# Attention and mixture-of-experts layer: the last output projection ahead of the fifth group's routing, its residual and statistics ahead of the early search, the early ranks behind the last transposes

## The reference

```
x = x + cross_attention(layernorm(x), context, mask)     # 16 heads of 16, projected by Wo, plus bo
n = layernorm(x)                                         # 1792 rows of 256
gate_probs = softmax(n @ router_w)                       # 8 experts
topk_w, topk_idx = top_k(gate_probs, 2); topk_w /= sum   # two experts for each row
x = x + sum over the two of  weight * (silu(n @ w1[e]) @ w2[e])      # 256 -> 512 -> 256
```

## Time and profile before

| | |
|---|---|
| time, median of 3 runs | 452.66 us (452.36 to 453.35) |
| the profiled execution's own time | 451.87 us |
| its span, first to last instruction | 449.9 us |
| TensorE busy, weight loads busy | 411.5 us (91%), 382.5 us (85%) |
| VectorE, ScalarE, GpSimd busy | 336.4 us (75%), 279.8 us (62%), 223.9 us (50%) |
| share of TensorE in the chain that ended last | 79% |
| share of VectorE, of DMA in it | 9%, 5% |
| mean clock granted to TensorE | 0.959 of full |

### The profile page before, as it was taken

How to read it: one execution, slowest core, us unless ns; L and a number is a source line. 1 busy time by engine, 2 the same in 40 slices (tenths; PEclk the granted TensorE clock), 3 DMA queues, 4 the chain that set the end, 5 groups by cost and what they waited for, 6 DMA issues and landing times.

```text
span 449.9 us, 10827 instructions
## 1 busy us (share of the span) xinstructions
PE 411.5 (91%) x4219; PEld 382.5 (85%) x4219; DVE 336.4 (75%) x700; ACT 279.8 (62%) x381; POOL 223.9 (50%) x257
## 2 busy tenths in 40 slices
PE   7878999999999999999999996899999999999910
PEld 6747898999989999999998985789999999999910
DVE  7866778778877888787788778856886667776536
ACT  4767476665566665766555554648778777778600
POOL 6757443312444223433202764675787878876420
PEclk9999999999999999999999997589999999999975
DMA  7995676768866778766450259822222322332169
GB/s 213 237 199 155 135 158 131 150 150 162 197 159 156 153 140 189 157 132 128 96 120 3 75 205 365 272 68 73 85 80 85 95 83 94 83 82 73 47 231 306
DMA packets 44675, 64.32 MB, mean 143 GB/s; under 512 B 6801, under 2 KB 33570, under 8 KB 44626
## 3 DMA queue, kind: packets, MB, share of 16 engines
q1 hardware_dynamic: 38322, 50.40, 45.6%
q0 software_dynamic: 4096, 11.13, 8.2%
q10 hardware_dynamic: 2208, 2.12, 1.4%
HBM read 30.13 MB, written 9.28 MB: 88 GB/s over the span
## 4 chain that ended last, share of the span: by engine, by line
PE 79%; DVE 9%; DMA 5%; ACT 3%; issue 2%; POOL 1%; ACTq 0%; SPq 0%; DVEq 0%
PE ps L1546 41%; PE ps L1609 12%; PE ps L1626 9%; PE ps L1640 9%; PE ps L1915 2%; DVE x L1536 2%; PE ps L1653 2%; DMA q_stack<-attn_t_lo 1%; DMA y_back<-y_rows 1%; DVE neg_max L1105 1%; DMA keep<-keep_scratch 1%; PE ps L1709 1%; DMA keep_scratch<-keep_all 1%; PE ps L1665 1%; PE ps L1719 1%
## 5 line engine op out<-in xcount | busy, mean ns | idle before, releaser
L1105 DVE TENSOR_REDUCE neg_max<-ps 112x1 f32<-112x376 f32 x256 | 133.6, 545 | 41.4 <-PE ps L1609 36.5
L834 ACT ACTIVATE probs<-ps 125x1344 f32<-125x1344 f32 x64 | 82.8, 1294 | 43.4 <-PE ps L1626 38.2
L1609 PE MATMUL ps<-k_stack,q_stack 98*112 98x376 f32 x256 | 86.2, 369 | 3.7 <-DVE neg_max L1105 2.2
L604 POOL TENSOR_TENSOR k_lo<-k_f,k_hi 128x752 fp32r<-128x752 f32 x16 | 28.9, 1806 | 112.3 <-ACT k_hi L808 111.8
L765 POOL DMA_INDIRECT rows<-xn_rows,token_of_row x42 | 55.8, 1328 | 17.5 <-issue 12.5
L773 POOL DMA_INDIRECT y_rows<-y_out,slot_of_row x42 | 45.6, 1087 | 25.3 <-ACT y_out L1027 14.4
L1609 PEld LDWEIGHTS ps<-k_stack,q_stack 98*112 98x112 f32 x256 | 44.1, 174 | 16.3 <-DVE neg_max L1105 10.9
L1626 PE MATMUL ps<-q_stack,k_stack 100*125 100x224 f32 x384 | 52.6, 273 | 0.0
L1626 PEld LDWEIGHTS ps<-q_stack,k_stack 100*125 100x125 f32 x384 | 50.4, 188 | 0.7 <-ACT probs L834 0.5
L1546 PE MATMUL ps<-w_hi,h_hi 128*128 128x256 f32 x168 | 48.8, 290 | 0.4 <-DVE h_lo L1452 0.4
L1546 PE MATMUL ps<-flat_t_hi,w_hi 128*128 128x256 f32 x168 | 47.5, 283 | 1.3 <-DVE flat_t_lo L1430 1.3
(11 more groups left out here) (213 smaller groups left out, 1017.6 us busy)
## 6 DMA issues: line engine op xcount, KB each, us to landing
k_stack<-k_hi SPq DMA_DIRECT2D x32, 376.0 KB, 5.0
w_all<-w SPq DMA_DIRECT2D x2, 4096.0 KB, 18.8
k_stack<-k_lo SPq DMA_DIRECT2D x16, 376.0 KB, 5.5
ctx_raw<-ctx_t SPq DMA_DIRECT2D x32, 187.5 KB, 3.9
q_stack<-attn_t_hi SPq DMA_DIRECT2D x64, 56.0 KB
y_back<-y_rows SPq DMA_DIRECT2D x14, 256.0 KB, 5.1
x_rows_sb<-x_rows SPq DMA_DIRECT2D x4, 448.0 KB, 4.6
x<-x_tiles SPq DMA_DIRECT2D x7, 256.0 KB, 2.9
```

The costliest lines, as they stand in the source:

```text
L604: pool.tensor_tensor(kl[:, :, :], kf[:, :, :], kh[:, :, :].bitcast(F32), ALU.subtract)\
L834: act.activation(pf[j % 2][:, :, :], ps[0:CT, BK_ST:BK_ST + KT, 0:4 * S], ACT.Exp).then_inc(pf_ready, 1)
L1105: dve.tensor_reduce(neg_max[:, head:head + 1], ps[0:S, BK_MAX + s % 2, 0:CP], AX.X, ALU.max, negate=True).then_inc(max_read, 1)
L1609: pe.matmul(ps[0:S, BK_MAX + a, 0:CP], qs[b.ring][0:R_MAX, a, q, :], ks[b.ring][0:R_MAX, q, :], start=True, stop=True).then_inc(smax_done, 1)
```

## The change

Three calls are moved, on two engines; no instruction is added or taken away. On VectorE's list `residual(7)` and `row_vars(7)` go from behind `find_two(early)` to ahead of it, and `normalise_late(7)` from behind `flat_low(6)` to right behind `find_two(early)`, ahead of `flat_low(5)`. On TensorE's list `project_output(7)` goes ahead of `route(4)`, and `rank_early` goes behind `flat_transpose(7)`, which puts `route(5)` and `flat_transpose(7)` ahead of it.

```diff
@@ VectorE
             attn_low(last)
             read_logits(3)
-            find_two(early_tiles, 4)
             residual(7)
             row_vars(7)
+            find_two(early_tiles, 4)
+            normalise_late(7)
             flat_low(5)
             flat_low(6)
-            normalise_late(7)
             place_rows(0, early_tiles, BK_RANK)
             flat_low(7)
             read_logits(4)
@@ TensorE
             attn_transpose(last)
             route(3)
             flat_transpose(5)
+            project_output(7)
             route(4)
-            project_output(7)
             flat_transpose(6)
-            rank_early()
             route(5)
             flat_transpose(7)
+            rank_early()
             route(6)
             route(7)
             rank_late()
```

## The result

The changed kernel takes 457.08 us (median of 4 runs, 456.27 to 457.46); the kernel before took 452.55 us beside it (452.36 to 453.35). The ratio is 1.0094 with an interval of 1.0076 to 1.0113: 4.5 us slower by the medians, 0.9% (4.3 us) by the ratio. 457.4 us was forecast, within 455.4 to 458.5. The profiled execution took 456.27 us with a span of 454.3 us; before, 451.87 and 449.9.

What follows compares the result with a forecast made beforehand. The hand-over was taken as one chain of dependent steps through VectorE's list: 5.06 us later placing less 0.29 gives 4.8 us, 456.7 by the profiled execution, 457.4 as a median, range 455.4 to 458.5.

Steps and rivals of the forecast that it cites:

- Step 1: TensorE's list: the projection of unit 7 starts at 269.98; the fourth routing comes 0.8 us later and costs nothing.
- Step 2: VectorE's list: 0.9 us idle before the residual; the early search starts at 272.17 in place of 270.12.
- Step 3: Fifth low part and routing: the routing starts at 276.52, 1.16 us later; VectorE could begin placing at 276.72.
- rival D: Early placing: VectorE comes later than the ranks, so only 0.55 us is lost, 453.2 us; chance 0.01.
- Step 4: Early ranks behind routing and transposes: the early placing starts at 280.94 in place of 275.88, 5.06 us later.
- Step 5: Last low part: VectorE's 0.29 us wait for ScalarE's high part goes, net 4.8 us there and at the end.
- The last sign in the prediction: Prediction wrong if some of the shift at the early placing is gone again by the filling of the lanes.
- Rival C: TensorE in the hand-over: the clock never falls, 0.4 us slower, 453.0 us; chance 0.04.
- Rival A: TensorE from 276.52 on: the clock comes back in the unbroken work, 3.4 to 4.4 us slower; chance 0.17.
- Rival B: Early search on VectorE: it loses time to GpSimd's root, 5.0 to 5.4 us slower; chance 0.09.

Runs made afterwards that it cites:

- e8: The kernel before with only TensorE's projection of unit 7 moved ahead of the fourth routing: 451.95 us beside 451.89, ratio 1.0007.
- e1: The changed kernel with the early ranks put back ahead of the fifth routing, the other moves kept: 454.65 us beside 452.59, ratio 1.0040.
- e2: The kernel before with only the early ranks moved behind the last transposes: 455.90 us beside 452.59, ratio 1.0073.
- e5: The changed kernel with nine more unread products of 48 columns right ahead of the early ranks: 457.97 us beside 451.89, ratio 1.0137.
- e7: The changed kernel with 18 unread products in TensorE's idle stretch ahead of the fifth routing: 455.02 us beside 451.89, ratio 1.0073.
- e3: The changed kernel with 34 unread products between the sixth transposes and the fifth routing: 456.62 us, ratio 1.0094.
- e6: The changed kernel with VectorE's last low part put ahead of the early placing and its wait: 456.24 us beside 451.89, ratio 1.0091.
- e9: The kernel before with few unread products (2, 5, 1, 10, 2 and 2) in TensorE's gaps: 453.87 us beside 452.87, ratio 1.0007.

## Why the prediction was right, point by point

Step 1, the projection: expected at 269.98 in the frame of before, it is at 270.58 - 0.57 = 270.01, and e8 shows no cost of moving it alone.

Step 2, the residual ahead of the search: 0.9 us of idle time, measured 0.99; the search at 272.17, measured 272.22.

Step 3: the fifth routing at 276.52, measured 276.60. The trace bears the step out; its neighbour, rival D, does not stand. I put 0.55 us on the case in which the ranks do not hold the placing up. e1 is that case, and cost 1.8. What failed in D was to take the placing for the only thing on the path, and to let the 0.29 us before the last low part count as something that goes. It goes only if the ranks are late; if not, the 1.2 us by which the routing is later come through the high part to the last low part in full, and 0.6 more where the routing runs at the lower clock. The rows had it: the releaser of those 0.29 us is ScalarE's high part, which follows the fifth routing.

Step 4, the ranks behind the transposes: the placing at 280.94, measured 281.04, with the lower clock over all of it. e2 (3.3 us by this move alone) and e5 (every added product counts in full) show the mechanism, and e7's trace beside the changed kernel's the two prices, 2.9 and 4.8.

Step 5: 4.8 us at the last low part, measured 4.80; 4.78 at the reading of the lanes; 4.79 at the first expert products. From there on I had forecast the length of before; it came out 1.0 us shorter in one execution and 0.4 longer in the other. The last sign in the prediction, some of the shift at the placing gone again by the lanes, is met to the letter (5.16 us at the placing, 4.78 at the lanes) and contradicts step 5, which takes 0.29 off itself; beyond that 0.1 is gone.

That the 4.8 came out so closely is in part luck. The sum compares a routing wholly at the lower clock with one that lost its clock inside, since that is what the one trace of before had. Beside e8, whose clock fell ahead of the routing, the changed kernel is 4.2 us later at the last low part and 4.4 at the lanes. The medians say 4.5 to 4.7, the ratios 3.4 to 6.1 with their intervals.

The clock was forecast at the right level for a reason that holds in part. I said that it falls because TensorE stands idle ahead of the routing. It fell in the changed kernel, twice, within such a stretch (275.9 and 274.8), and with 18 fillers in it the clock stayed up until 279.5 in e7's execution. But in e2, e3, e5, e6 and e9 it fell between 269.6 and 270.8, ahead of the idle stretch, when TensorE was issuing routings, transposes and the projection with hardly a gap. So no idle stretch is needed for a fall. What causes the early one is not shown: up to 269.6 the order of work is the same in all 13 traces, behind it only the projection and the fourth routing change places, and the falls came with either order (TensorE busy for 1.80 of 2.00 us from 268 to 270 and 2.00 in the next two in the trace of before, which kept its clock there; 1.79 and 2.00 in e6's, which lost it at 269.7), and in five traces only. Why the clock falls at 270 in some executions and at 276 in others stays open, and with it whether the idle stretch or what came before it brought the fall in the changed kernel. Rival C, no fall at all, was seen in none of the 13 traces.

Rival A, the clock coming back inside the unbroken run of work behind the gap, did not happen in the changed kernel: the granted clock is 0.50 in every window from 276 to 299. Rival B did not cost VectorE anything: the first operation of the search took 0.69 us with the root beside it, as before. The root took 0.95 us in place of 0.56. The Trainium skill ("SBUF — State Buffer", Who interferes with whom) has the one that starts second wait, and here that was GpSimd (root at 272.95, search at 272.79); the trace agrees, and I had looked at it from the wrong side. It cost nothing, since the root was needed at 276.10 only.

## What to carry to other kernels

A step that runs in a gap of its engine costs nothing there; before it is moved behind something, ask when its reader will want it and what stands behind that reader. Here the ranks ran free at 272.6, their reader came at 275.9, and the move put them behind a routing that could not start before 276.5. And where two waits end close to each other, as the placing's operands and the high part did, price each as if the other were gone: e1 kept the ranks early, the high part was the bound, and it cost 1.8 us where 0.55 had been forecast. Ask also where the clock fell in the trace that the prices are read from: with the same order on VectorE, e8's last low part came 0.6 us later than before's.

## What the runs showed of the hardware

- TensorE's clock fell from 1.00 to 0.50 between 269.6 and 279.5 in all 13 traces, at a place that changed from execution to execution of like kernels, and in five of them without an idle stretch ahead of it. The same work ahead of 269.6 was followed by a fall in five traces and by none before 274.7 in eight. Nine small products took 1.37 us above and 2.34 below.
- Products whose result nobody reads are no safe way to hold it up: 34 that take 0.117 us each at the full clock took 6.2 us when the clock had already fallen, and came out beyond the gap that they were to fill.
- A fall of the clock ahead of the change moves everything behind it: the projection's result came 0.3 to 1.0 us later in e3, e5 and e6 than in the changed kernel (idle time before the residual of 1.30, 1.39 and 1.95 us, against 0.99). A distance between two instructions of one trace told more than the medians of 12 runs did, once the place of the fall was read beside it.
